# Loading w1 before w2 and placing tokens with four token tiles' strips as weights, in a two-layer mixture-of-experts and state-space kernel

## The reference

```python
x = x + 0.5 * moe(layernorm(x))
x = x + ssm(layernorm(x))
x = x + 0.5 * moe(layernorm(x))
# moe: 8 experts, 160 places each
logits = tokens @ gate_w; probs = softmax(logits); expert = argmax(probs)
pos = cumsum(one_hot(expert)) - 1            # token's place in its expert, dropped from 160 on
h = relu(expert_input @ w1[e])               # 160x128 @ 128x512
out = probs[expert] * (h @ w2[e])            # back to the token
# ssm: h_t = ifft(lambda * fft(h_(t-1))) + B u_t ;  y = h C^T + D u
```

## Time and profile before

| | us |
|---|---|
| three runs | 153.84, 154.50, 155.39 (median 154.50) |
| profiled execution | 155.39 |
| its span in the trace | 153.2 |
| TensorE products busy | 135.3 (88%) |
| VectorE busy | 88.6 (58%) |
| ScalarE busy | 57.4 (37%) |
| GpSimd busy | 54.3 (35%) |

### The profile page before, as it was taken

The page is one execution under the profiler, slowest core; times in us unless marked ns, Lnnn a source line. Parts: engine busy times, 40 slices in busy tenths (PEclk is TensorE's granted clock), DMA queues, the critical chain, the costliest instruction groups (busy, mean ns, idle before and its releaser), DMA issues.

```text
span 153.2 us, 2526 instructions
## 1 busy us (share of the span) xinstructions
PE 135.3 (88%) x784; PEld 103.0 (67%) x784; DVE 88.6 (58%) x384; ACT 57.4 (37%) x141; POOL 54.3 (35%) x87
## 2 busy tenths in 40 slices
PE   5897999999999969579999999999979899999810
PEld 2324476368999946239888778878874399899700
DVE  1078796954446541276877978999882243554220
ACT  2513410444583406055564656451100145742200
POOL 3440000777205777101311221122002777027770
PEclk9999995599999999999999999999996999999995
DMA  4999999111100111690011011101011111001110
GB/s 121 282 357 386 369 486 415 39 51 51 34 0 17 58 51 54 199 327 28 0 68 45 23 73 68 70 1 68 4 68 68 51 51 51 21 0 51 54 51 17
DMA packets 11308, 16.21 MB, mean 106 GB/s; under 512 B 1664, under 2 KB 6272, under 8 KB 11264
## 3 DMA queue, kind: packets, MB, share of 16 engines
q1 hardware_dynamic: 9504, 13.11, 24.2%
q0 software_dynamic: 1280, 2.62, 5.5%
q10 hardware_dynamic: 512, 0.33, 0.9%
HBM read 12.65 MB, written 5.51 MB: 118 GB/s over the span
## 4 chain that ended last, share of the span: by engine, by line
PE 43%; issue 12%; DVE 11%; DMA 11%; POOL 10%; ACT 5%; SPq 4%; POOLq 1%; DVEq 0%
PE pair L965 9%; PE pair L976 7%; PE pair L907 7%; DMA w1s<-w 5%; POOL xg L326 4%; PE pair L1043 4%; ACT u L466 3%; SPq L267 2%; PE pair L934 2%; POOL out L335 2%; PE pair L863 2%; POOL x_scratch L335 2%; PE pair L1034 2%; DMA x<-x_scratch 2%; DVE sstat L737 2%
## 5 line engine op out<-in xcount | busy, mean ns | idle before, releaser
L863 PE MATMUL pair<-warm_in,ones_bf 128*128 128x512 bf16 x70 | 20.3, 437 | 3.3 <-DMA x<-x_scratch 1.7
L976 PE MATMUL pair<-hT,w2s 128*128 128x160 f32 x128 | 20.4, 302 | 0.2 <-ACT hT L414 0.2
L965 PE MATMUL pair<-xcT,w1s 128*128 128x160 f32 x128 | 20.5, 303 | 0.0
L414 ACT ACTIVATE hT<-pair 128x320 f32<-128x320 f32 x32 | 14.0, 438 | 15.2 <-PE pair L965 13.5
L965 PEld LDWEIGHTS pair<-xcT,w1s 128*128 128x128 f32 x128 | 18.0, 190 | 1.2 <-ACT xcT L406 0.8
L976 PEld LDWEIGHTS pair<-hT,w2s 128*128 128x128 f32 x128 | 17.9, 190 | 0.4 <-issue 0.2
L326 POOL DMA_INDIRECT xg<-x,tok x10 | 10.2, 1020 | 19.9 <-issue 19.9
L863 PEld LDWEIGHTS pair<-warm_in,ones_bf 128*128 128x128 bf16 x70 | 7.5, 112 | 13.1 <-issue 4.7
L326 POOL DMA_INDIRECT xg<-out,tok x10 | 10.1, 1012 | 13.6 <-DVE tok L671 10.8
L678 DVE BATCH_NORM_STATS2 gstat<-xg 128x6 f32<-128x128 f32 x20 | 5.8, 290 | 14.2 <-DMA xg<-out,tok 10.3
L335 POOL DMA_INDIRECT x_scratch<-xnew,tok x10 | 9.9, 993 | 10.8 <-DVE xnew L715 9.0
(11 more groups left out here) (181 smaller groups left out, 245.0 us busy)
## 6 DMA issues: line engine op xcount, KB each, us to landing
xt<-x_turned SPq DMA_DIRECT2D x8, 256.0 KB, 5.9
w1s<-w SPq DMA_DIRECT2D x2, 1024.0 KB, 7.4
w2s<-w SPq DMA_DIRECT2D x8, 256.0 KB, 6.7
x<-x_scratch SPq DMA_DIRECT2D x8, 256.0 KB, 4.3
out<-x SPq DMA_DIRECT2D x8, 256.0 KB, 2.0
ce<-const_early ACTq DMA_DIRECT2D x1, 318.0 KB, 4.7
cl<-const_late SPq DMA_DIRECT2D x1, 256.0 KB, 5.5
xg<-x,tok POOLq DMA_INDIRECT x10, 2.5
```

Source lines behind the costliest of these rows:

```text
L414: nc.scalar.activation(hT[:, e % 2, half * HC:(half + 1) * HC, :], bank[4 + half][:, 0:HC * CAP] .rearrange("p (c s) -> p c s", c=HC), ACT ...
L863: M(bank[to][:, :], ones_bf[:, :], warm_in[:, :], start=True, stop=True)
L965: ins = M(bank[4 + half][:, c * CAP:(c + 1) * CAP], w1s[:, i, ch * P:(ch + 1) * P], xcT[:, i * CAP:(i + 1) * CAP], start=True, stop=True)
L976: ins = M(bank[6 + i % 2][:, 0:CAP], w2s[:, i, c, :], hT[:, i % 2, c, :], start=(c == 0), stop=(c == FC - 1))
```

## The change

w1's second half is issued before w2. TensorE centers experts 2 to 5 before the placing, expert 6 within it and expert 7 behind it; the eight warming products ahead of it are gone.

The first placing takes four token tiles (a batch) at a time. VectorE's `encode_four` writes the token codes in the order group, strip, tile (`four_tok`), and `place_four` uses the 20 x 4 = 80 columns of a group as weights, with the 64 x 4 = 256 columns of `hot_place` for the same tiles as the moving side: 8 products in place of 32. Of the 80 x 256 result only those entries count in which the row's tile is the column's tile. `own_places` multiplies it by a mask (`own_tile`) into `spread`, and `place_own` adds the four up and turns them into the old table, in four products with `sum_strips` (which puts rows 4s to 4s+3 into strip s). VectorE does `index` before `lagged_inputs`, and TensorE waits for `xj_r` ahead of the first w2 product, which writes the bank that `lagged_inputs` reads. GpSimd prepares `strip_four` in eight copies, `sum_strips`, and `token_half` ahead of `strip_no`. The early constants have 24 more columns. In `choose`, in both MoEs, the last operation writes in the order of memory and reads in steps; before, it was the other way round.

```diff
@@ -67,6 +67,7 @@
         ident, sines = part(P), part(P)
         before_p, after_p = part(P), part(P)
         rev, iota_place, iota_strip, token_code = part(E), part(SW), part(NSTRIP), part(NT)
+        own_tile, own_strip = part(TB), part(NSTRIP)
         basis_in, basis_out, basis_turned = cl[:, 0:2 * P], cl[:, 2 * P:3 * P], cl[:, 3 * P:4 * P]
         ident_bf = sb("ident_bf", [P, P], BF16)
         before_bf = sb("before_bf", [P, P], BF16)
@@ -112,6 +113,11 @@
         slot_i = sb("slot_i", [P, NT], I16)
         split_i = sb("split_i", [P, 2, NT], I16)
         hot_place = sb("hot_place", [P, SW, NT], F16)
+        strip_four = sb("strip_four", [P, NT // TB, NSTRIP, TB], I16)
+        four_strip = sb("four_strip", [P, NT // TB, NSTRIP, TB], F16)
+        four_tok = sb("four_tok", [P, NT // TB, NSTRIP, TB], F16)
+        sum_strips = sb("sum_strips", [NSTRIP * TB, NSTRIP], F16)
+        spread = sb("spread", [NSTRIP * TB, SW, TB], F16)
         hot_strip = sb("hot_strip", [P, NSTRIP, NT], F16)
         hot_tok = sb("hot_tok", [P, NSTRIP, NT], F16)
         unfilled = sb("unfilled", [SW, NSTRIP])
@@ -214,6 +220,7 @@
 
         marked, ranked, rank_read, hot, placed, indexed = (sem(n) for n in ("marked", "ranked", "rank_read", "hot",
                                                                             "placed", "indexed"))
+        four_placed, spread_r = sem("four_placed"), sem("spread_r")
         w1c_ps, w1c_sb = sem("w1c_ps"), sem("w1c_sb")
         rated, slotT_ps, slotT_sb, slot_logits = (sem(n) for n in ("rated", "slotT_ps", "slotT_sb", "slot_logits"))
         gsd_r, lg_r, pe_r = (sem(n) for n in ("gsd_r", "lg_r", "pe_r"))
@@ -272,6 +279,7 @@
             for i in range(2):
                 h = slice(i * E // 2, (i + 1) * E // 2)
                 sp.dma_start(w1s[:, h, :], w1[h].rearrange("e d f -> d e f")).then_inc(d_w1[i], 16)
+            for i in range(2):
                 for e in range(i * E // 2, (i + 1) * E // 2):
                     sp.dma_start(w2s[:, e, :, :], w2[e].rearrange("(c p) d -> p c d", p=P)).then_inc(d_w2[i], 16)
             sp.dma_start(x1_dram, x_rows).then_inc(d_fill, 16)
@@ -307,8 +315,12 @@
             nc.gpsimd.tensor_copy(before_bf[:, :], before_p)
             nc.gpsimd.tensor_copy(after_bf[:, :], after_p)
             nc.gpsimd.tensor_copy(ident_bf[:, :], ident).then_inc(pool_set, 1)
+            nc.gpsimd.tensor_copy(token_half[:, :], token_code)
+            nc.gpsimd.tensor_copy(sum_strips[:, :], own_strip[0:NSTRIP * TB, :])
+            for g in range(NT // TB):
+                ins = nc.gpsimd.tensor_copy(strip_four[:, g, :, :], iota_strip.unsqueeze(2).broadcast_to([P, NSTRIP, TB]))
+            ins.then_inc(pool_set, 1)
             nc.gpsimd.tensor_copy(strip_no[:, :, :], iota_strip.unsqueeze(2).broadcast_to([P, NSTRIP, NT]))
-            nc.gpsimd.tensor_copy(token_half[:, :], token_code).then_inc(pool_set, 1)
             nc.gpsimd.memset(xg[:, :, :], 0.0).then_inc(pool_set, 1)
             pool.wait_ge(gate_sb, 1)
             nc.gpsimd.tensor_copy(eye_gate[:, 0:D], ident)
@@ -583,8 +595,9 @@
                 link(V.tensor_tensor(key[:, ts, :], is_top[:, ts, :],
                                      rev_bf[:, :].unsqueeze(1).broadcast_to([P, wd, E]), ALU.mult))
                 link(V.reduce_max(top_key[:, ts], key[:, ts, :], axis=AX))
-                return V.tensor_tensor(chosen[n][k][:, :, t0 - first:t0 - first + wd].rearrange("p e t -> p t e"),
-                                       key[:, ts, :], top_key[:, ts].unsqueeze(2).broadcast_to([P, wd, E]), ALU.is_equal)
+                return V.tensor_tensor(chosen[n][k][:, :, t0 - first:t0 - first + wd],
+                                       key[:, ts, :].rearrange("p t e -> p e t"),
+                                       top_key[:, ts].unsqueeze(1).broadcast_to([P, E, wd]), ALU.is_equal)
 
             def mark(n, k, parts=(True, True)):
 
@@ -650,6 +663,22 @@
                 V.tensor_tensor(hot_tok[:, :, ts], hot_strip[:, :, ts],
                                      token_half[:, ts].unsqueeze(1).broadcast_to([P, NSTRIP, wd]), ALU.mult)
 
+            def encode_four():
+
+                def by_four(a):
+                    return a.rearrange("p (g t) -> p g t", t=TB).unsqueeze(2).broadcast_to([P, NT // TB, NSTRIP, TB])
+
+                link(V.tensor_tensor(four_strip[:, :, :, :], by_four(split_i[:, 1, :]), strip_four[:, :, :, :], ALU.is_equal))
+                V.tensor_tensor(four_tok[:, :, :, :], four_strip[:, :, :, :], by_four(token_half[:, :]), ALU.mult)
+
+            def own_places():
+
+                dve.wait_ge(four_placed, 1)
+                V.tensor_tensor(spread[:, :, :],
+                                bank[7][0:NSTRIP * TB, 256:256 + SW * TB].rearrange("p (s t) -> p s t", t=TB),
+                                own_tile[0:NSTRIP * TB, :].unsqueeze(1).broadcast_to([NSTRIP * TB, SW, TB]),
+                                ALU.mult).then_inc(spread_r, 1)
+
             def encode_place(n, k):
 
                 for t0, t1 in hot_parts(n, k):
@@ -721,10 +750,11 @@
             dve.wait_ge(pool_set, 1)
             mark(0, 0)
             number(0, 0)
-            encode(0, 0)
+            encode_four()
             encode_place(0, 0)
+            own_places()
+            index(0)
             lagged_inputs()
-            index(0)
             carried_table()
             powers(ct, st, 0, 5)
             slots(0)
@@ -926,6 +956,23 @@
                 M(flat, ident_bf[:, :], counted[n][k][:, :, :].rearrange("p e t -> p (e t)"),
                   start=False, stop=True).then_inc(ranked, 1)
 
+            def place_four():
+
+                for part_no, (t0, t1) in enumerate(hot_parts(0, 0)):
+                    pe.wait_ge(hot, part_no + 1)
+                    for t in range(t0, t1, TB):
+                        ins = M(bank[7][0:NSTRIP * TB, 256:256 + SW * TB],
+                                four_tok[:, t // TB, :, :].rearrange("p s t -> p (s t)"), hot_place[:, :, t:t + TB],
+                                start=(t == 0), stop=(t == NT - TB))
+                ins.then_inc(four_placed, 1)
+
+            def place_own():
+
+                pe.wait_ge(spread_r, 1)
+                for t in range(TB):
+                    ins = M(bank[7][0:SW, 0:NSTRIP], spread[:, :, t], sum_strips[:, :], start=(t == 0), stop=(t == TB - 1))
+                ins.then_inc(placed, 1)
+
             def place(n, k):
 
                 for part_no, (t0, t1) in enumerate(hot_parts(n, k)):
@@ -967,6 +1014,8 @@
                                         start=True, stop=True)
                             ins.then_inc(h_ps, 1)
                     elif kind == "d":
+                        if n == 0 and i == 0:
+                            pe.wait_ge(xj_r, 1)
                         if n == 0 and i % (E // 2) == 0:
                             pe.wait_ge(d_w2[i // (E // 2)], 16 * (E // 2))
                         pe.wait_ge(h_sb, n * 2 * E + 2 * i + 2)
@@ -1004,11 +1053,12 @@
             pe.wait_ge(pool_set, 1)
             center_w1(0, 2)
             rank(0, 0)
-            center_w1(2, E // 2)
+            center_w1(2, E - 2)
+            place_four()
+            center_w1(E - 2, E - 1)
+            place_own()
+            center_w1(E - 1, E)
             pe.wait_ge(gg_sb, 1)
-            keep_warm(8, 4)
-            place(0, 0)
-            center_w1(E // 2, E)
             keep_warm(4, 4)
             slots(0)
 
@@ -1150,7 +1200,7 @@
         eye, sines,
         (n[:, None] < n[None, :]).astype(float), (n[:, None] > n[None, :]).astype(float),
         np.tile(E - np.arange(E), (P, 1)), np.tile(np.arange(SW), (P, 1)), np.tile(np.arange(NSTRIP), (P, 1)),
-        token_code], axis=1)
+        token_code, n[:, None] % TB == np.arange(TB), n[:, None] // TB == np.arange(NSTRIP)], axis=1)
     q = np.arange(P // 2)
     cos = np.cos(2 * np.pi * ((n[:, None] * q[None, :]) % P) / P)
     sin = np.sin(2 * np.pi * ((n[:, None] * q[None, :]) % P) / P)
```

## The result

The changed kernel took 156.5 us (median; 156.37 to 156.85), the one before 154.48 us (153.84 to 155.39): 1.0144 times as long, 95% interval 1.0107 to 1.018. The forecast was 153.5 us. The profiled execution took 156.85 us, its span 155.0 us.

A forecast was written before the change was run, and what follows sets the result against it. TensorE's centering, partly at half clock, was taken to bound the head, with the gather close beside it. 155.39 - 2.8 (earlier expert 0) + 1.5 (low clock) - 0.55 (choice operation) = 153.5 us; range 152.1 to 155.1 us.

The forecast's parts named there:

- Placing, encodings, mask, centering in the pauses: First placing: new encodings, fewer products, mask and interleaved centering start index at 23.45 instead of 24.59 us, 1.1 us gained.
- a landing later than 15.1 us: Head: sign against the prediction, w1's first half landing after 15.1 us, which would move everything; its landing was taken as unchanged.
- A gather lands 2.5 us after its issue: First gathers: issued at 25.4 and 26.9 us, they land at 27.9 and 29.4 us.
- The later start is TensorE's centering, not the gather: Head of the kernel before: both tiles are there by 30.5 us, but centering holds expert 0 until 32.97 us.
- the 2.8 us forecast for expert 0's start: First MoE: earlier gathers let expert 0 start at 30.1 instead of 32.9 us.
- 0.68 set: First MoE: 0.68 us from the second tile's transpose to expert 0's first product, taken from the second placing.
- Its last piece still lands where it did, since the bytes ahead of it are the same: Head's loads: w2's last piece lands at an unchanged time despite w1's second half going first; w2 is wanted after 30 us.
- The clock: First experts: TensorE idles waiting for gathers, its clock falls to 1.2 GHz and takes 1.5 us back.
- the one taken: First experts: a low-clock stretch of 3.4 us beginning around 29 to 30 us; lasting twice as long was a sign against.
- the second rival: Head: the clock stays low 6.5 us or more, costing 2.5 instead of 1.5 us; 154.5 us, chance 0.17.
- The choice operation: Second placing: chosen takes 0.34 instead of 0.70 us, twice; 0.55 us gained on the path, bounds 0 and 0.8.
- the slower one: First experts: low clock lasts until expert 2's dense products, 8.5 us of work costing 4.25 us; 156.3 us, chance 0.07.

The follow-up runs named there:

- e1: Changed kernel with 28 instead of 4 warming products ahead of its first slots: 154.45 us, 1.0019 times the kernel before.
- e14: Changed kernel with a 416-byte padding tile, w2's second half issued only after gather 9 landed, and 16 warming products: 152.66 us, 0.9886 times the kernel before.
- e10: Changed kernel with an unused 416-byte tile between early and late constants: 155.7 us, 1.0081 times the kernel before.
- the two other pairs with and without the tile: The 416-byte padding tile added to e1, giving e11: 154.45 to 153.48 us; added to e17, giving e15: 155.61 to 153.89 us.
- e2: Changed kernel with the copy of x into the scratch issued only after the second gather landed: 160.59 us, 1.0452 times the kernel before.
- e15: Changed kernel with a 416-byte padding tile and 24 small products in the wait for x1 after the first MoE: 153.89 us, 0.9992 times the kernel before.
- e19: e14 with 4 instead of 16 warming products: 154.34 us, 1.0026 times the kernel before.
- e7: Changed kernel with the copy of x into the scratch issued directly behind w1, ahead of w2: 156.69 us, 1.0158 times the kernel before.
- e17: Changed kernel with 24 small products in the wait for x1 after the first MoE, without a padding tile: 155.61 us, 1.0073 times the kernel before.
- e11: Changed kernel with a 416-byte padding tile and 28 instead of 4 warming products: 153.48 us, 0.9949 times the kernel before.
- e13: Changed kernel with a 416-byte padding tile, w2's second half issued only after gather 4 landed, and 16 warming products: 155.04 us (153.24 to 159.89).
- e16: Kernel before with w2's second half issued behind gather 9, after the copy of x: 154.39 us, 1.0004 times the kernel before.

## Why the prediction was wrong

- *Placing, encodings, mask, centering in the pauses*: right. The index came 0.76 us earlier; the forecast was 1.1. What is missing is w1's later landing (0.33 us), taken as unchanged; the prediction had named a landing later than 15.1 us as a sign that it was wrong. The landing varies by more than that between traces (14.8 to 15.6 us), so it can be chance.
- *"A gather lands 2.5 us after its issue"*: the step that failed. It gave the first gather 27.9 us and expert 0 30.1 us; they were 30.66 and 32.67 us. The 2.5 us are the median of ten; the view of this tile in the kernel before also has the longest:

```profile
DMA to landing us min/median/max: 2.4/2.5/3.5
```


  The first gather took 3.5 us, landing at 30.05 us, 0.2 us behind the copy of x (29.85 us), and TensorE's centering hid it. "The later start is TensorE's centering, not the gather" was true, but behind it stood the queue, not a gather that would follow the index. In the changed kernel the copy was done at 30.44 us: of the 2.8 us forecast for expert 0's start 0.3 came. The 2.6 us from 30.1 to 32.67 us are, by the second tile, which expert 0 also needs: 0.4 us for the later issue (27.27 instead of 26.9 us), 1.1 us for the queue (3.57 instead of 2.5 us from issue to landing), 0.2 us for the way from landing to product at the full clock (0.93 us in e1, 0.68 set), and 0.9 us for the low clock on that way. The queue also lengthened TensorE's wait and, as the item on the clock argues, with it the low stretch; so its share is probably larger than 1.1 us. e14 shows the early start once the queue is lightened and the clock is kept.
- *"Its last piece still lands where it did, since the bytes ahead of it are the same"*: the bytes were, the rate was not. w2's last piece landed at 25.6 us, before at 23.7 us. The 24 columns of constants were priced at 0.03 us for their bytes; by moving every later tile by 96 bytes they cost 0.8 us (e10; 1.0 and 1.7 us in the two other pairs with and without the tile).
- *The clock*: it fell as forecast, and in the idleness named. The stretch was 6.8 us, twice the one taken, which the prediction had named as a sign that it was wrong. TensorE idled for 5.0 instead of 2.8 us: in the traces with a wait of 2.8 to 3.7 us for the first gather (e2, e15, e19) the stretch was 3.4 us, in those with 4.3 to 5.4 us (the changed kernel, e7, e10, e17) 6.8 us. It cost 1.2 us between expert 0 and expert 1 and another 0.9 us before expert 0, from the second gather's landing to its start (1.83 us, in e1 0.93 us): 2.1 us in all, for which 1.5 was set. So the second rival, a low clock of 6.5 us or more, came true as a mechanism; its 154.5 us had neither the late gather nor the late store in it.
- *The choice operation*: priced right (0.38 against 0.34 us). Of the 0.55 us on the path only 0.17 arrived: from va at 95.44 us to own_count at 111.79 us there are 16.35 us, before 16.52 (94.55 to 111.07). The first saving shortened one round by 0.15 us (5.63 us from va to va instead of 5.78), and the second ended in front of TensorE, which ranks behind add_rows.
- *Missing altogether*: that taking away 28 of TensorE's matmuls and their 28 weight loads (the trace has 756 of each instead of 784) moves its code fetch onto the last output store: 0.9 us (e17).

The sum with what was measured: 155.39 - 0.3 (expert 0's start, with the clock's 0.9 us in it) + 1.2 (clock from there on) - 0.17 + 1.05 (store) = 157.2 against 156.85 us. Of the rivals, the slower one's 156.3 us was near the result by chance: its mechanism, 8.5 us of work at the low clock, wasn't there. By medians the loss is accounted for: 156.5 - 0.9 (fetch) - 0.8 (alignment) - 1.15 (clock, the rest of e1's 2.05) = 153.65, and e11, which removes all three, has 153.48. These are medians of different chips; that the terms add up is supported by this one sum.

What stays open: why e15 gained 0.8 us more than the store, what in the tile's start makes the packets slower, and the size of the alignment's cost in the kernel before.

## What to carry to other kernels

Before a stage is moved earlier, ask for each transfer that it waits for when the last of its kind landed and what stood ahead of it in every queue; a median duration hides the one that counts. Where an engine will wait for data in place of working, put warming work there in the same edit. And a changed tile size or instruction count shifts everything behind it, so after an unexplained loss a padding tile or a few idle instructions are cheap tests.

## What the runs showed of the hardware

- First gathers issued while SyncE's queue still held the end of its loads took 3.2 to 5.6 us, and 2.7 to 2.8 us with the queue drained (e2, e13, e14, e16, e19). The copy's packets (32 of 64 KB) last 2.4 to 2.9 us each on average, in the changed kernel 2.45 us. The Trainium skill, "DMA: Bandwidth & Descriptors", section "Queues, rings and completion order", has an engine alternate between its queues packet by packet. The copy is compatible with that; e7, with only 512-byte packets of 31 ns in front and a first gather of 5.3 us, does not follow from it, if what the trace lists as a packet is what the page means.
- 512-byte packets into SBUF last 27 to 28 or 31 to 32 ns, at 346 to 351 or 290 GB/s, depending on where the tiles start: slow when moved by 96 or 416 bytes, fast when not moved or moved by 512.
- A 16 KB code fetch of 1.3 us that began 0.2 us behind the issue of a 256 KB store made it land 1.05 us late (3.03 instead of 1.98 us). Moving the fetch by 24 small products took 1.0 us off the store and 0.9 us off the kernel's time (e17).
